# A decoder layer on one core: the keys-first pass of the attention runs ten slots behind the queries-first pass instead of nine

## Time and profile before

| what | value |
|---|---|
| median of three runs | 1187.57 us |
| the profiled execution, its own time | 1182.92 us |
| its span (first to last instruction) | 1181.1 us |
| mean granted PE clock | 0.955 of full |
| PE busy | 1036.4 us (88%) |
| DVE / ACT / POOL busy | 665.4 / 534.9 / 667.2 us |
| instructions | 22568 |
| `mixing`, `routing` with `experts` | about 0 to 514 us, then to the end |

### The profile page before, as it was taken

How to read it: one execution, slowest core, us unless ns; L and a number is a source line. 1 busy time by engine, 2 the same in 40 slices (tenths; PEclk the granted TensorE clock), 3 DMA queues, 4 the chain that set the end, 5 groups by cost and what they waited for, 6 DMA issues and landing times.

```text
span 1181.1 us, 22568 instructions
## 1 busy us (share of the span) xinstructions
PE 1036.4 (88%) x6564; PEld 874.2 (74%) x6564; DVE 665.4 (56%) x2184; ACT 534.9 (45%) x1179; POOL 667.2 (56%) x808
## 2 busy tenths in 40 slices
PE   4689999999999998740799999999999999999980
PEld 3568877778787876430588888888888888888880
DVE  4577777777777776317444454344544444544427
ACT  1255555555455555420444554444545445545431
POOL 5456665666566665411536566566565565565453
PEclk8899999999999999875799999999999999999995
DMA  5333333333333222041335453455453454544348
GB/s 157 101 99 92 94 98 101 86 107 98 91 90 90 72 64 65 19 152 58 117 93 112 110 119 58 107 120 103 110 105 68 111 115 107 115 75 94 46 79 260
DMA packets 91184, 116.89 MB, mean 99 GB/s; under 512 B 14049, under 2 KB 66402, under 8 KB 90978
## 3 DMA queue, kind: packets, MB, share of 16 engines
q1 hardware_dynamic: 64370, 81.71, 23.2%
q0 software_dynamic: 24576, 33.57, 17.2%
q10 hardware_dynamic: 2160, 0.78, 0.3%
HBM read 65.41 MB, written 29.36 MB: 80 GB/s over the span
## 4 chain that ended last, share of the span: by engine, by line
PE 41%; DVE 4%; issue 3%; ACT 2%; DMA 1%; POOL 0%; ACTq 0%; DVEq 0%; SPq 0%; POOLq 0%
PE y_bank L1124 15%; PE gate_bank L1124 12%; PE value_bank L1124 12%; PE turn_bank L1134 2%; DVE w_lo L1260 2%; ACT w_hi L1192 1%; DVE hidden L1279 1%; DMA acc_rows<-y,slots_now 1%; DVE last L1303 1%; DVE stats L1310 1%; DMA raw<-in_w 0%; DVE xT_lo L1265 0%; DVE mv L1314 0%; POOL acc_rows L1087 0%; ACT y L1217 0%
## 5 line engine op out<-in xcount | busy, mean ns | idle before, releaser
L1087 POOL DMA_INDIRECT acc_rows<-y,slots_now x128 | 209.4, 1636 | 186.6 <-ACT y L1217 164.7
L1279 DVE TENSOR_TENSOR hidden<-gate,value_bank 128x512 f32<-128x512 f32 x128 | 88.0, 687 | 253.6 <-ACT gate L1226 235.7
L731 DVE CUSTOM_DVE_ANT_0 scored<-score,band 128x178 f32<-128x178 f32 x512 | 153.1, 338 | 80.3 <-PE score L443 69.6
L605 ACT ACTIVATE probsT<-scoreT 128x356 f32<-128x356 f32 x256 | 117.8, 470 | 169.8 <-PE scoreT L471 77.9
L1226 ACT ACTIVATE gate<-gate_bank 128x512 f32<-128x512 f32 x128 | 76.6, 598 | 221.9 <-PE value_bank L1124 221.9
L1068 POOL DMA_INDIRECT rows<-x_rows,rows_now x128 | 136.8, 1069 | 60.0 <-issue 46.2
L1124 PE MATMUL y_bank<-w_hi,h_hi 128*128 128x256 f32 x512 | 146.5, 286 | 0.0
L1124 PE MATMUL y_bank<-w_hi,h_lo 128*128 128x256 f32 x512 | 144.4, 282 | 0.0
L1124 PE MATMUL y_bank<-w_lo,h_hi 128*128 128x256 f32 x512 | 144.0, 281 | 0.0
L443 PE MATMUL score<-k_stack,q_stack 96*128 96x178 f32 x512 | 123.1, 323 | 6.7 <-DMA q_stack<-low_q 4.2
L471 PE MATMUL scoreT<-q_stack,k_stack 97*128 97x356 f32 x256 | 114.8, 449 | 0.0
(11 more groups left out here) (149 smaller groups left out, 2327.2 us busy)
## 6 DMA issues: line engine op xcount, KB each, us to landing
raw<-in_w SPq DMA_DIRECT2D x48, 512.0 KB
k_stack<-high_k SPq DMA_DIRECT2D x128, 64.0 KB, 2.2
q_stack<-high_q SPq DMA_DIRECT2D x128, 64.0 KB, 2.4
xin<-in_x SPq DMA_DIRECT2D x16, 256.0 KB, 3.0
xT<-in_xT SPq DMA_DIRECT2D x16, 256.0 KB, 3.2
cT<-in_cT SPq DMA_DIRECT2D x16, 256.0 KB, 3.7
k_stack<-low_k SPq DMA_DIRECT2D x64, 64.0 KB, 2.2
q_stack<-low_q SPq DMA_DIRECT2D x64, 64.0 KB, 2.3
```

The costliest lines, as they stand in the source:

```text
L605: nc.scalar.activation(probsT[g % 2][:, u % HG, :, :].rearrange("p a s -> p (a s)"), scoreT[u % 2][:, 0:2 * SPAN], ACT.Exp, scale=1.0 / DH ...
L731: op = nc.vector.tensor_tensor_reduce(scored[t % 2][:, q, :], score[t % 2][:, q * SPAN:(q + 1) * SPAN], band[:, q, :], -1.0, BIG, ALU.add, ...
L1087: nc.gpsimd.indirect_dma_start(dram["acc"][c], bass.IndirectOffsetOnAxis(ap=slots_now[it.r % 2][:, c:c + 1], axis=0), y[m][:], None, compu ...
L1279: nc.vector.tensor_tensor(hidden[f % 2][:], gate[f % 2][:], value_bank[f % 2][:], ALU.mult).then_inc(hidden_ready, 1)
```

## The change

The constant `LAG` goes from 9 to 10, and what follows from the keys-first pass moves with it by one slot: `gather` from slots 2, 6, 10, 14 to 3, 7, 11, 15; the spreading of the sums from 3, 7, 11, 15 to 0, 4, 8, 12 (the first of them in the next step); `invert_sums` from 0, 4, 8, 12 to 1, 5, 9, 13; the multiplication into `attnT` from 2, 6, 10, 14 to 3, 7, 11, 15. `turn_maxima` and `keep_maxima` stay at 1, 5, 9, 13, and so does every projection and everything of the layernorms. The order of POOL and of SP within a step is not edited. No instruction is added or taken away.

```diff
-LAG = 9
+LAG = 10
...
             def gather(it, t):
 
-                g = group(t, 14)
+                g = group(t, 15)
...
                     turned_heads(it, t)
-                    if t in (2, 6, 10, 14):
+                    if t in (3, 7, 11, 15):
                         gather(it, t)
...
             def invert_sums(it, t):
 
-                g = group(t, 16)
+                g = group(t, 17)
...
-                    if t in (0, 4, 8, 12):
+                    if t in (1, 5, 9, 13):
                         invert_sums(it, t)
...
-                    if t % 4 == 3 and has(it, group(t, 15)):
+                    if t % 4 == 0 and has(it, group(t, 16)):
 
-                        g = group(t, 15)
+                        g = group(t, 16)
                         dve.wait_ge(attn_ready, it.lin(NG, g + 1))
                         met()
                         nc.vector.stream_shuffle(sums[g % 2][:], attn[g % 2][:, 0:S], sums_from).then_inc(sums_ready, 1)
-                    if t % 4 == 2 and it.batch(-1):
+                    if t % 4 == 3 and it.batch(-1):
 
-                        g = group(t, 18)
+                        g = group(t, 19)
                         dve.wait_ge(inverse_ready, it.lin(NG, g + 1))
```

## The result

The changed kernel takes 1229.33 us (median of 4 runs, 1223.1 to 1235.6) against 1187.74 us of the kernel before (4 runs, 1187.45 to 1188.78): a ratio of 1.0349, 95% interval 1.0296 to 1.0402. The direction was forecast, the size was not: +41.6 us where I had +21.2, and the time lies outside the range of 1196.5 to 1220. The profiled execution is the quickest of the four, 1223.1 us with a span of 1221.3. The four runs differ in their mean granted clock: 0.946, 0.941, 0.939 and 0.940 go with 1223.1, 1229.5, 1235.6 and 1229.2 us.

The account below looks back on a forecast made before the run. PE sets the pace, busy 26.70 of 28 us. Steps 2 to 13 add 16.8 us, steps 14 and 15 4.8, the ends -0.4: 21.2 us more, 1208.8 us by the median, range 1196.5 to 1220.

Parts of the forecast that it names:

- The late Ln and Exp of group -2: ACT slot 9: Ln and Exp behind exponential 9, rough 3.7 us later, rstd_O 2.45 later, so x2cur and PE late.
- The gather's hole in slot 11: PE ahead of slot 11's scores: hole of 0.26 becomes about 0.97 us; 0.7 per step if nothing later absorbs it.
- The step is 1.4 us longer: Steps 2 to 13 of mixing: next heads(0) at about 174.75 against 173.33; 12 x 1.4 = 16.8 us.
- Step 15 and the drain: Last step and drain, up to the router's next product: 2.9 us longer, of which step 15 itself 2.4.
- Rival E: PE's clock falls as its stands grow: 3.2 us per step, 45 more, 1254 us; chance 0.02.
- slots 2 and 3, and 6 and 7, exchange the gather at no cost: PE early in the step: moving the gather out of slot 6 costs nothing, as slot 5's exponential is ready in time.
- Ln and Exp of groups -4, -3 and -1: Other groups' inverses: group -4 starts about 2.9 us later, but nothing in slots 0 to 10 reaches PE.
- the wider distance to the maxima's DMAs: Longer lag before the maxima's DMAs: brings nothing, since no wait of PE ends by them.
- A: Rival: DVE or POOL has more room, only slot 11's uncovered 0.7 us per step stays: 1197.6 us; chance 0.12.
- B: Rival: ACT in slots 13 to 15 sets the end and is freed, 12.8 us less: 1174.8 us; chance 0.08.
- C: Rival: all is hidden within 0.2%, needing slack of 2.4 us in the O chain: 1187.6 us; chance 0.05.
- D: Rival: group -4's late inverse delays Q's rotation and exponential 8, up to 1 us per step: 14 more, 1223; chance 0.06.

Follow-up runs that it names:

- experiment 1: Changed kernel with ACT's Ln and Exp of group -2 put back in slot 8: 1211.41 us (1.0203).
- experiment 2: Kernel before, lag left at 9, with only Ln, Exp and DVE's multiplication a slot later: 1218.59 us (1.0264).
- experiment 5: Changed kernel with O's estimate on ACT ahead of Ln and Exp, and its refinement on POOL ahead of group -2's inverse: 1229.29 us in one run.
- experiment 3: Changed kernel plus overwritten filler matmuls on PE, ahead of slot 11's keys-first scores and while waiting for x2cur in slot 13: 1223.93 us (1.0306).
- experiment 4: Kernel before with Ln, Exp and the multiplication a slot later, plus overwritten filler matmuls on PE in slot 13: 1208.97 us (1.0174).
- experiment 8: Changed kernel (lag 10) with ACT's exponentials, Ln, Exp and estimate ahead of the maxima's DMA issues, and x2T ahead of slot 13's issues: 1198.45 us (1.0070).
- experiment 9: Changed kernel (lag 10) with exponentials ahead of the maxima's DMA issues and Ln and Exp of group -2 back in slot 8: 1191.05 us (1.0016).
- experiment 6: Kernel before with ACT's copy of x2T ahead of the exponential in slot 14: 1181.47 us (0.9947).
- experiment 7: Kernel before with ACT's exponentials ahead of the maxima's DMA issues, and x2T ahead of exponential 14: 1166.10 us (0.9819).

## Why the prediction was wrong

- *The late Ln and Exp of group -2* and its chain over POOL and DVE to PE: right in place and nearly in time (6.52 against 6.4 to `rstd_O`, PE's transposes 7.73 after the turn of the maxima where I had 7.7). Shown by experiment 1 (taken back: the wait at line 509 goes) and 2 (alone: it comes). Incomplete in its road: experiment 5 shows a second one by DVE's multiplication.
- *The gather's hole in slot 11*: I had 0.97 us ahead of the keys-first scores, behind ACT alone. Measured are 0.52 behind DVE and 0.40 behind ACT. Together they are 0.92, so the size was right. But the prediction has no wait of `heads(11)` for the maxima of slot 9, and that wait is why no order of ACT that was tried here cures lag 10.
- *"The step is 1.4 us longer"*: measured 1.8. A term mis-sized by 0.4, over 12 steps 4.8 us. Of the 0.4, 0.13 is that I started from a step of 28.33 where most are 28.2; 0.13 is that I gave R 0.65 up to the next `heads(0)` where the earlier trace rows show 0.78 (172.55 to 173.33); and 0.14 is that `heads(15)` comes 27.79 after `heads(0)` where I had 27.65. Step 15 and the drain took 6.6 against 2.9; the clock falls there too (0.87 granted from 490.36 to 517 us), and I have not split that sum.
- *Rival E, the clock, dismissed with 0.02.* This is the step that failed: the sum has no term for the clock. I wrote "My longest new stand is about 1.3 us, far under 4.82, so this is unlikely". In steps 1 to 14 of the profiled execution no stand is longer than 1.3, and the clock fell all the same in steps 1, 2, 4, 5 and 9, steps that are 10.6 us longer together. About 9.4 of that is the clock's: in experiment 3 steps 1 and 2 keep 1.00 and are still 0.3 and 1.0 longer than the kernel before and than a clean step. Without these 9.4 the median of 1229.3 would be about 1220, the upper end of the range; the terms below their measured size, of the step and of step 15 with the drain, fill the rest. I compared the longest single stand, where the changed kernel has four in slots 11 to 15 of a step (0.52, 0.40, 0.94, 0.74). The kernel before had a single one of 1.51 in step 1 and kept 1.00. Experiments 2 and 4 show cause and cure where the falls are regular.

  What picks a step is open. In the changed kernel the falls are not regular: step 3 has 0.51, 0.41, 1.06 and 0.74 and keeps 1.00, step 4 has 0.52, 0.40, 0.94 and 0.74 and doesn't. The sum of the stands is not what decides either: a step of experiment 1 has 2.0 us of them, in four of 0.36 to 0.56, and keeps 1.00, and a step of experiment 2 has 1.9, of which 0.6 and 1.1 stand close together, and loses it nearly every time.

  The 6 us between the profiled execution and the median go with the clock: of the four runs, the quickest has the highest granted clock and the slowest the lowest. The kernel before spreads as much on the chips of the experiments (1181 to 1194), so the spread is no mark of the change.

  The rule of the Trainium skill that I weighed ("TensorE: Matmul & The Clock Gate", Part 1) speaks of longer idle gaps; for stands as short as these the measurement decides. A later section of the same part ("A second HAM failure mode: psum-queue depth-cycling") tells of a kernel whose short repeated idle times between groups of matmuls make the clock swing, and the traces of the changed kernel and of experiment 2 agree with it: 0.97 and 0.95 granted from 84 to 420 us.
- *Right*: slots 2 and 3, and 6 and 7, exchange the gather at no cost; Ln and Exp of groups -4, -3 and -1 don't reach PE; the wider distance to the maxima's DMAs brings nothing. Rivals A to D fell in the trace. PE waits at line 509 and the steps are 30.0 (against A); its idle time per step is 2.6 us where it was 1.3 (against B and C); and the copy of the maxima of slot 9 comes 18.32 after `heads(0)` as before (against D).

## What to carry to other kernels

Before moving a stage, ask of each engine what it does in the time that the moved piece covered, not only of the engine that is waited for now; and follow what the moved piece then stands behind on its own in-order engine (here 1.2 us of DMA issues), and who stands behind it on the next ones. On a kernel bound by TensorE, look at all its stands in a step and how close together they are, not only at the longest: in experiment 2 the waits cost 1.05 us per step and the clock behind them about 1.2 more. Put what an engine computes for others ahead of the DMAs that it issues, where these have time: with `x2T` moved forward as well, that gave 1.8% here.

## What the runs showed of the hardware

- The granted clock fell behind short stands of PE: in experiment 2 behind one of 0.59 and one of 1.02 us. Three matmuls of 128x512 more in each step take most of the falls away (0.95 to 0.99) and cost less than they bring (1218.59 to 1208.97 us). In the changed kernel (experiment 3) such matmuls bring no gain of the total that is clear of noise.
- Where the second and the third trip of the loop begin, an engine stops for 2 to 3.5 us with no releaser. In the kernel before it is ACT and DVE, at both places. In experiments 3, 4, 8 and 9 it is PE at both, in experiments 2, 6 and 7 at one of the two, and the clock then falls as well: the two steps around such a start take up to 7 us more than two clean ones (about 2 in the kernel before). Experiments 6 to 9 add nothing to PE's list, so it is not the filler. What decides on which engine the stop falls stays open.
- An activation ahead of two DMA issues on ACT runs beside them, one behind them waits until they are done. In the kernel before, the exponential behind the issues starts 1.67 us after the copy ahead of them (163.32 to 164.99). In experiment 7 the exponential is listed ahead of the issues, and both start together; the next activation starts 0.1 us behind the end of the issues (ACTq):

```profile
159.92 0.47 ACT L605 ACTIVATE probsT<-scoreT 128x356 f32<-128x356 f32 x1
...
159.92 1.21 ACTq L628 DMA_DIRECT2D q_stack<-nmaxT  x2
...
161.25 0.20 ACT L85 ACTIVATE log_O<-mv_O 128x2 f32<-128x2 f32 x1 [0.87 <-issue]
```
